# Two chunks of a layer's experts run as one stream of slot tiles, with a wait for GpSimd's second transfer of a step

## The reference, cut to what is computed

```python
x = x + linear_cumsum(layernorm(x))             # 8 sequences of 512 tokens, 128 wide
x = x + experts(layernorm(x))                    # 8 experts, 2 for each token
x = x + local_attention(layernorm(x))            # 16 heads, window of 128
x = x + experts(layernorm(x))                    # the same weights once more

# experts(x): xn = normalised x
probs = softmax(xn @ router_w.T / 1.5); w, idx = top_k(probs, 2)
h = silu(xn @ W1[e]);  y = h @ W2[e]             # 128 -> 512 -> 128
out = sum of w * y over the two experts, + x
```

## Time and profile before

| | |
|---|---|
| time of the kernel before | 985.13 us, median of 3 runs (983.61 to 986.66) |
| the profiled execution | 979.9 us, of which the span between first and last instruction is 977.8 us |
| PE busy | 684.0 us (70%) |
| DVE busy | 611.0 us (62%) |
| POOL busy | 435.3 us (45%) |
| ACT busy | 408.3 us (42%) |

### The profile page before, as it was taken

One profiled execution on the slowest core, in us unless ns is written; L12 is line 12 of the kernel. 1 busy time (PEld: TensorE's weight loads), 2 busy tenths in 40 slices (PEclk: granted clock), 3 DMA queues, 4 the chain that ended last, 5 costly groups with the idle time before them and its releaser, 6 DMA issues.

```text
span 977.8 us, 30500 instructions
## 1 busy us (share of the span) xinstructions
PE 684.0 (70%) x11616; PEld 523.8 (54%) x11616; DVE 611.0 (62%) x1840; ACT 408.3 (42%) x691; POOL 435.3 (45%) x409
## 2 busy tenths in 40 slices
PE   3811767797657677988888988877576777566770
PEld 2511556575545554655655656655375556455560
DVE  7888797854454557656656565677678544354444
ACT  1370245353333342754654655655354334233340
POOL 6591573484655600112122100050576766666661
PEclk9999977999988899999998999967767988798886
DMA  7210012132222221221211201001021111233114
GB/s 221 68 33 0 25 23 81 48 64 56 65 56 76 72 73 36 62 61 30 72 46 45 70 26 36 6 19 28 17 69 39 44 45 39 66 83 102 56 39 137
DMA packets 62923, 54.61 MB, mean 56 GB/s; under 512 B 10129, under 2 KB 55954, under 8 KB 62778
## 3 DMA queue, kind: packets, MB, share of 16 engines
q1 hardware_dynamic: 53250, 33.12, 11.8%
q0 software_dynamic: 9536, 19.55, 8.0%
HBM read 31.79 MB, written 20.84 MB: 54 GB/s over the span
## 4 chain that ended last, share of the span: by engine, by line
PE 43%; DVE 29%; issue 12%; another core or an unknown queue 6%; DVEq 4%; ACT 3%; DMA 2%; POOL 1%; SPq 0%; ACTq 0%; POOLq 0%
PE stbank L1109 6%; PE bank L1212 4%; PE stbank L1096 4%; PE sbank L1170 3%; DVE gl L767 3%; PE stbank L1110 3%; PE stbank L1098 3%; DVE zr L586 3%; DVE mx L825 2%; PE sbank L1165 2%; PE stbank L1196 2%; PE stbank L1097 2%; DVE ysb L757 2%; DVE xs L783 2%
## 5 line engine op out<-in xcount | busy, mean ns | idle before, releaser
L478 POOL DMA_INDIRECT xg<-table,idx x156 | 159.1, 1020 | 162.8 <-PE sbank L1077 66.4
L903 ACT ACTIVATE g<-stbank 128x512 f32<-128x512 f32 x156 | 93.3, 598 | 316.1 <-PE stbank L1098 242.5
L1109 PE MATMUL stbank<-wff,gh 128*128 x624 | 142.3, 306 | 112.0 <-DVE ysb L757 74.5
L757 DVE TENSOR_REDUCE ysb<-stbank 128x128 f32<-128x256 f32 x156 | 65.9, 423 | 152.4 <-remote 88.5
L1096 PE MATMUL stbank<-xT,wff 128*128 128x128 f16 x624 | 148.8, 246 | 17.3 <-issue 9.7
L825 DVE TENSOR_REDUCE mx<-sbank 128x2 f32<-128x320 f32 (+1 forms) x256 | 116.1, 472 | 68.6 <-PE sbank L1170 61.4
L950 ACT ACTIVATE pT<-stbank 128x1024 f32<-128x1024 f32 (+1 forms) x128 | 116.8, 917 | 81.4 <-PE stbank L1196 80.2
L1098 PE MATMUL stbank<-xT,wff 128*128 128x128 f16 x624 | 149.1, 246 | 0.0
L1097 PE MATMUL stbank<-xT,wff 128*128 128x128 f16 x624 | 146.5, 242 | 0.0
L1109 PEld LDWEIGHTS stbank<-wff,gh 128*128 128x128 f16 x624 | 67.5, 108 | 144.3 <-issue 126.6
L1110 PE MATMUL stbank<-wff,gl 128*128 x624 | 130.2, 239 | 0.0
(11 more groups left out here) (188 smaller groups left out, 1334.0 us busy)
## 6 DMA issues: line engine op xcount, KB each, us to landing
yslot<-ysb SPq DMA_DIRECT2D x78, 64.0 KB
table<-tb SPq DMA_DIRECT2D x16, 256.0 KB
cg<-ytab SPq DMA_DIRECT2D x16, 256.0 KB
qz<-dumps SPq DMA_DIRECT2D x96, 32.0 KB
kst<-dumps SPq DMA_DIRECT2D x96, 32.0 KB
xg<-table,idx POOLq DMA_INDIRECT x156
xs<-in_x SPq DMA_DIRECT2D x8, 256.0 KB, 4.6
qz<-in_w SPq DMA_DIRECT2D x1, 2048.0 KB, 10.4
```

Source lines behind the costliest of these rows:

```text
L478: g.indirect_dma_start(xg[:, i % G].rearrange("p a d -> p (a d)"), None, table[cc % 2], bass.IndirectOffsetOnAxis(ap=idx[:, cc % 2, t:t + ...
L903: a.activation(g32[:, i % 3, :], hbank[i % 2], ACT.Silu, scale=1.0 / WSCALE)
L1109: mm(o, gh[:, i % 3, P * f:P * f + P], whl, start=(f == 0), stop=False, skip_group_check=True)
```

## The change

The steps of a layer are one run of 88 (`range(2 * XSTEPS)`), and `layer_tile(layer, n)` gives the n-th of the layer's 78 tiles. Tiles of the second chunk follow those of the first without draining and filling. They end in step 82 where they ended in step 87. What runs beside stays at its steps: `beside(layer, s - XSTEPS)` from step 44 on. Beside step number k stood tile k of the second chunk at the transposes; now stands tile k + 5. Apart from this POOL gets a wait, `tile_under_way`: ahead of the scatter of a step (layer 1) and of the gather back of a step (layer 0) it waits for `s_h` of tile s-3, that is the end of the up projection that PE issues in step s-1.

```diff
@@ -205,6 +205,11 @@
         def tile_of(cc, t):
             return SLOT_TILES * cc + t
 
+        def layer_tile(layer, n):
+
+            i = tile_of(CHUNKS * layer, n)
+            return (i, i // SLOT_TILES, i % SLOT_TILES) if 0 <= n < CHUNKS * SLOT_TILES else (None, None, None)
+
         def scattered(slot, end):
 
             return (end - 1 - slot) // G - (tile_of(CHUNKS, 0) - 1 - slot) // G
@@ -239,16 +244,15 @@
 
 
             c0 = CHUNKS * layer
-            for s in range(XSTEPS):
-                x_step(c0, s)
-                if layer == 0:
+            for s in range(2 * XSTEPS):
+                x_step(layer, s)
+                if s >= XSTEPS:
+                    beside(layer, s - XSTEPS)
+                elif layer == 0:
                     a_step(1, s)
                     r_step(c0 + 1, s - A_BEFORE_R)
                 else:
                     r_step(c0 + 1, s)
-            for s in range(XSTEPS):
-                x_step(c0 + 1, s)
-                beside(layer, s)
 
         def front_in_attention(front, b, j):
...
+            def tile_under_way(layer, s):
+
+                i, _, _ = layer_tile(layer, s - 3)
+                if i is not None:
+                    pool.wait_ge(s_h, i + 1)
+
+            def x_step(layer, s):
+                if layer == 0 and ZERO_AT <= s < ZERO_AT + ZEROS:
 
                     if s == ZERO_AT:
                         pool.wait_ge(s_wl, 2)
@@ -467,23 +476,24 @@
                     n = 3 * NH * SEQ // ZEROS
                     z = qz[:].rearrange("p u h n -> p (u h n)")[:, n * (s - ZERO_AT):n * (s - ZERO_AT + 1)]
                     g.memset(z.bitcast(F32), 0.0).then_inc(s_zero, 1)
-                if s == 0:
-                    pool.wait_ge(s_idx, cc + 1)
-                    for i in range(2):
-                        pool.wait_ge(s_tbd[i], 16 * 2 * (cc + 1))
-                for t in range(AHEAD + 1) if s == 0 else (s + AHEAD,):
-                    if t < SLOT_TILES:
-                        i = tile_of(cc, t)
-                        wait(pool, s_xp, i - G + 1)
-                        g.indirect_dma_start(xg[:, i % G].rearrange("p a d -> p (a d)"), None, table[cc % 2],
-                                             bass.IndirectOffsetOnAxis(ap=idx[:, cc % 2, t:t + 1], axis=0)).then_inc(s_g[i % G], 16)
-
-                for t in (s - 6,) if s < XSTEPS - 1 else (s - 6, s - 5):
-                    if cc >= CHUNKS and t >= 0:
-                        i = tile_of(cc, t)
-                        pool.wait_ge(s_yc, i + 1)
-                        g.indirect_dma_start(ytab[cc % 2], bass.IndirectOffsetOnAxis(ap=sidx[:, cc % 2, t:t + 1], axis=0),
-                                             ysb[:, i % G, :], None).then_inc(s_sc[i % G], 16)
+                for n in range(AHEAD + 1) if s == 0 else (s + AHEAD,):
+                    i, cc, t = layer_tile(layer, n)
+                    if i is None:
+                        continue
+                    if t == 0:
+                        pool.wait_ge(s_idx, cc + 1)
+                        for k in range(2):
+                            pool.wait_ge(s_tbd[k], 16 * 2 * (cc + 1))
+                    wait(pool, s_xp, i - G + 1)
+                    g.indirect_dma_start(xg[:, i % G].rearrange("p a d -> p (a d)"), None, table[cc % 2],
+                                         bass.IndirectOffsetOnAxis(ap=idx[:, cc % 2, t:t + 1], axis=0)).then_inc(s_g[i % G], 16)
+
+                i, cc, t = layer_tile(layer, s - 6)
+                if layer and i is not None:
+                    tile_under_way(layer, s)
+                    pool.wait_ge(s_yc, i + 1)
+                    g.indirect_dma_start(ytab[cc % 2], bass.IndirectOffsetOnAxis(ap=sidx[:, cc % 2, t:t + 1], axis=0),
+                                         ysb[:, i % G, :], None).then_inc(s_sc[i % G], 16)
 
             def gather_back(b, m):
 
@@ -507,6 +517,7 @@
             def beside(layer, s):
                 m = gathered_back_at(s)
                 if layer == 0 and m is not None:
+                    tile_under_way(layer, XSTEPS + s)
                     gather_back(m // GATHERS, m % GATHERS)
                 if layer == 0 and prepared_at(s):
                     front(*prepared_at(s))
...
@@ -746,22 +757,22 @@
                     dve.drain()
                     v.tensor_tensor(sidx[:, cp, :], row, far, ALU.add).then_inc(s_idx, 1)
 
-            def x_step(cc, s):
-                if 0 <= s - 5 < SLOT_TILES:
-                    i = tile_of(cc, s - 5)
+            def x_step(layer, s):
+                i, _, _ = layer_tile(layer, s - 5)
+                if i is not None:
                     dve.wait_ge(s_y, i + 1)
                     if i - G < tile_of(CHUNKS, 0):
                         wait(dve, s_ys[i % G], 16 * (i // G))
                     else:
                         dve.wait_ge(s_sc[i % G], 16 * scattered(i % G, i))
                     v.tensor_reduce(ysb[:, i % G, :], ybank.rearrange("p (a d) -> p d a", a=2), AX.X, ALU.add).then_inc(s_yc, 1)
-                if s < SLOT_TILES:
-                    i = tile_of(cc, s)
+                i, _, _ = layer_tile(layer, s)
+                if i is not None:
                     dve.wait_ge(s_xp, i + 1)
                     wait(dve, s_h, i - 2)
                     v.tensor_copy(xT[:, i % 3, :], xbank[i % 2]).then_inc(s_xt, 1)
-                if 0 <= s - 3 < SLOT_TILES:
-                    i = tile_of(cc, s - 3)
+                i, _, _ = layer_tile(layer, s - 3)
+                if i is not None:
                     dve.wait_ge(s_gh, i + 1)
                     wait(dve, s_y, i - 2)
                     v.tensor_tensor(gl[:, i % 3, :], g32[:, i % 3, :], gh[:, i % 3, :], ALU.subtract).then_inc(s_gl, 1)
...
@@ -1065,31 +1076,31 @@
                     if k == 16:
                         ins.then_inc(s_ixp, 1)
 
-            def x_step(cc, s):
-                if s == 0:
-                    pe.wait_ge(s_wl, 2)
-                    pe.wait_ge(s_idx, cc + 1)
-                if s < SLOT_TILES:
-                    i = tile_of(cc, s)
+            def x_step(layer, s):
+                i, cc, t = layer_tile(layer, s)
+                if i is not None:
+                    if t == 0:
+                        pe.wait_ge(s_wl, 2)
+                        pe.wait_ge(s_idx, cc + 1)
                     pe.wait_ge(s_g[i % G], 16 * (i // G + 1))
                     wait(pe, s_xt, i - 1)
                     for a2 in range(2):
                         ins = pe.transpose(xbank[i % 2][:, P * a2:P * a2 + P], xg[:, i % G, a2, :], ident16[:])
                     ins.then_inc(s_xp, 1)
-                if s % LOADS == 0 and s < SLOT_TILES:
-
-                    n = min(LOADS, SLOT_TILES - s)
-                    _, ids = nc.values_load_multi_w_load_instructions(
-                        eid[0:1, cc % 2, s:s + n], [mybir.EngineType.PE], min_val=0, max_val=E - 1,
-                        skip_runtime_bounds_check_because="a count of thresholds passed, cut off at E - 1")
-                    for k in range(n):
-                        experts[s + k] = wff[:, bass.ds(ids[k], 1), :, :]
-                if 0 <= s - 2 < SLOT_TILES:
-                    i = tile_of(cc, s - 2)
+                    if t % LOADS == 0:
+
+                        n = min(LOADS, SLOT_TILES - t)
+                        _, ids = nc.values_load_multi_w_load_instructions(
+                            eid[0:1, cc % 2, t:t + n], [mybir.EngineType.PE], min_val=0, max_val=E - 1,
+                            skip_runtime_bounds_check_because="a count of thresholds passed, cut off at E - 1")
+                        for k in range(n):
+                            experts[i + k] = wff[:, bass.ds(ids[k], 1), :, :]
+                i, _, _ = layer_tile(layer, s - 2)
+                if i is not None:
                     pe.wait_ge(s_xt, i + 1)
                     wait(pe, s_gh, i - 1)
...
```

23 lines of the change are left out of this document (10 added, 13 removed).

## The result

| | before | after |
|---|---|---|
| median | 985.89 us (4 runs, 983.61 to 986.94) | 972.01 us (4 runs, 965.77 to 974.98) |
| profiled execution, its span | 979.9, 977.8 us | 965.77, 963.7 us |

The ratio is 0.9863, with a 95% interval of 0.9828 to 0.9899: a gain of 13.9 us in the medians and 14.1 us between the two profiled executions, where 20.6 were forecast.

A forecast was written before the change was run, and what follows sets the result against it. Bound by waits: runs of POOL's transfers, 1.43 us each, keep others from seeing what PE finished. Layer 1's seam -5.2, layer 0 -9.4, new wait -6: -20.6 from 985.1 gives 964.5 us, range 954 to 975.

The forecast's parts named there:

- (c): Layer 0, steps 31 to 38: without gathers they take 23.9 us instead of 30.53; -6.6 us, bounds -14.5 and 0.
- (e): End of layer 0: the V projection loses its cover, so the mask comes later; +1.9 us, other end 5.
- part 3: New wait before gathers back and scatters: a tile takes 2.94 us instead of 3.015; -6 us, bounds 0 and -13.
- Part 1: Layer 1, seam between chunks goes: 39 tiles take 117.6 us as a stream instead of 122.82; -5.2 us.
- Part 2: Layer 0: the seam goes and the work beside meets other tiles; -9.4 us in sum.
- (a): Layer 0, step 5 of the second half: its reduce comes at 244.8 instead of 240.63; +4.2 us.
- (b): Layer 0, steps 5 to 30 of the second half: same work, 85.75 us, unchanged without the new wait.
- (d): End of layer 0: the last reduce stands in step 38 instead of 43; -8.9 us.
- The wait does nothing: Both layers: the new wait brings nothing, only the seams' removal counts; 970.5 us; chance 0.20.
- The wait breaks the hold: Two-transfer steps: finished PE work gets through between POOL's transfers, 2.55 us a tile; 932.5 us, halfway 949; chance 0.14.
- The wait delays the scatters: Layer 1: the reduce waits for the delayed scatter's landing, 3.74 us a tile; 1011.8 us; chance 0.11.
- The gain of layer 0 doesn't come: Layer 0: steps 31 to 38 save nothing and its end costs 5 us; +0.3 there, 974 us; chance 0.10.

The follow-up runs named there:

- The stream alone: The changed kernel without the new wait in either layer, only the run of 78 tiles; 977.91 us, ratio 0.9921 to the kernel before.
- the long fill: The changed kernel, but in layer 1 POOL fills 520 unused columns behind each scatter instead of waiting ahead of it; 966.53 us, ratio 0.9886.
- two fills: The changed kernel, but in layer 1 POOL fills 256 unused columns behind each gather and each scatter, without the wait; 968.48 us, ratio 0.9909.
- POOL's plain store: The changed kernel, but in layer 1 POOL stores each tile's rows without indices in the scatter's place; 915.18 us.

## Why the prediction was right, and where its sizes were wrong

The forecast was -20.6 us, the measurement -13.9. The sign, the mechanism of layer 0 and the range held. The range was wide: the bounds of (c), (e) and part 3 even add up to 950 to 980 us, not to the 954 to 975 given, so that it held is weak evidence for the steps. Step by step:

**Part 1, the seam of layer 1 (-5.2): mis-sized, about -1.** The term was 39 tiles at 3.015 us against 122.82. The 3.015 came from 26 tiles of one execution. The stream alone ran at 3.11 in tiles 15 to 29, where its program is still that of the kernel before, and the other kernels with two indexed transfers and no fill there at 3.04 to 3.15. The kernel before itself has 2.99 in these tiles: 3.015 was the low side of what executions scatter. With 3.11 the term is 121.3 - 122.8 = -1.5 us. With the seam put back, the ratio rises by 0.1%, which the intervals don't tell from nothing. The step that failed is the pace: 3.11 us for a tile where 3.015 was said, 0.1 us on each of 39 tiles.

**Part 2, layer 0 (-9.4): right, and larger.** Its own steps, with the wait's share in them:
- (a) said +4.2, with 11 tiles at 2.0 us. They took 24.95 us (223.01 to 247.96), 2.27 each: tiles 35, 39 and 43 took 3.0 us, seven of the other eight 1.9 to 2.0, the last 2.4. The three are the tiles whose down projections stand in the steps in which PE loads four expert numbers (`t % LOADS == 0`); that these loads cost the 1 us is likely, but no run varied them. So tile 44's reduce stands 7.3 us behind the 240.63 of the earlier trace rows.
- (b) said 85.75 us unchanged (and -1.9 of part 3). It took 81.8 (247.96 to 329.80), -3.9; without the wait 83.6 and 84.8.
- (c) said 23.9 us for steps 31 to 38. They took 21.8 (329.80 to 351.60), -8.7 in the place of -6.6; without the wait 25.4 and 24.1, about as said.
- (d), 8.9 us, falls away as said: 7.3 - 3.9 - 8.7 - 8.9 = -14.2.
- (e) said that the mask follows the last reduce by 2.3 us in the place of 0.49. It follows by 2.67 (351.60 to 354.27), +2.2 where +1.9 was said (the terms given add up to 2.0). The first scores follow by 4.66 us where it was 1.57 (365.77 to 367.34), +3.1. Here the granted clock of PE counts, which the forecast left out: PE was busy for 1.91 of the 4 us up to 352, then the clock fell to the lower of its two levels (0.50, 1.2 GHz), and the four mask products took 1.87 us in the place of 1.04. In the seven kernels of the stream whose mask takes 1.02 us the scores follow by 3.81 to 3.87 us, so +2.3 without the clock. The stacks, the other end of (e), cost nothing: the scores start 0.12 us behind the mask's end. The stretch up to layer 1 is 1.5 us longer here; it lasts 352.2 to 359.3 us in the twelve kernels with the stream in layer 0, 355.9 in the mean, and 352.9 and 349.4 in the two without. So some of what layer 0 wins may be lost again there, which two executions can't settle.

```profile
354.27 1.87 PE L1263 MATMUL stbank<-mband,ident 128*128 128x512 f16 x4
...
356.26 0.43 PE L1181 MATMUL sbank<-kst,qz 127*32 127x128 f16 x8
```

The same scores in the kernel before, and the stretch after in which the clock fell (us, busy us of PE, PEld, DVE, ACT and POOL, granted clock, DMA):

```profile
367.34 0.29 PE L1170 MATMUL sbank<-kst,qz 127*32 127x128 f16 x8
```

```profile
352.00:356.00 4.00, 3.13 (x11) 1.51 (x10) 1.16 (x5) 1.05 (x5) 0.00 (x0) 0.50 0.55 175
```

**Part 3, the new wait (-6): right in sum, its mechanism not confirmed.** It is worth 0.9921 - 0.9863 = 0.6%, 5 to 6 us, with intervals that overlap a little. But it was to come from 0.075 us on each of 82 tiles. In layer 1 (57 of them, -4.3) a round with the wait isn't shorter (6.1 to 6.25 us for two tiles, 3.1 each, where 2.94 was said), and the profiled executions show nothing; only the medians show 4 us there, and only without the wait of layer 0. In layer 0 the profiled executions show some 4 us where 1.9 was said, in the steps of (b) and, to my surprise, of (c), where POOL issues gathers back alone. In the kernel before it brought nothing in layer 0 (365.5 against 365.8). Why it works only beside the stream no run settles. That the sum came out near 6 is luck as far as its working goes.

**The rivals.** "The wait does nothing" is refuted for the whole; for layer 1 it is open. "The wait breaks the hold" fell: idle times of 3.5 us remain. "The wait delays the scatters" fell for this change, and came true with the long fill. "The gain of layer 0 doesn't come" fell.

**The rule that spoke against part 3.** With SP's plain store in the scatter's place, the same bytes land and a tile costs 2.04 in the place of 3.1 us. POOL's indexed transfers do hold what PE has finished. The Trainium skill ("SBUF — State Buffer", section "Who interferes with whom") says that PE and ACT never wait on anyone and that a DMA never contends with a compute engine. It speaks of ports of SBUF; the traces show only that others go on late after PE is done, not which part of the chip holds them. By its rule, as the prediction took it, the plain store would have gained nothing; the measurement decides against it.

## What to carry to other kernels

Count the transfers with index lists that POOL issues close behind each other, not their rows or bytes. In this kernel one alone held nothing back, while a run of them held what the matrix engine had finished for some 1.4 us each, up to the end of the run, and one fewer in a step was worth 1 us for each step. Merging two pipelines saves the seam only where the seam is slower than the stream: here the draining ran free of the hold, so in layer 1 nothing was won, and in layer 0 the win came from the seam's own steps and from tiles that now stand beside other work. And a pace read from 26 tiles of one execution is not good to 0.1 us; multiplied by 57 or 82 tiles, that is the whole forecast.

## What the hardware showed beside this

**The hold by the transfer.** 64 rows took 0.91 us to issue and 128 rows 0.99, and both held equally; a plain store issued by POOL took 0.58 us and held nothing; neither did an indexed transfer that stood alone.

**A transfer that starts while DVE subtracts is longer.** In the kernel with the fill of 520 columns the subtraction (`gl`, two inputs in SBUF) began at 802.11 and the scatter at 802.20:

```profile
802.11 0.68 DVE L783 TENSOR_TENSOR gl<-g,gh 128x512 f16<-128x512 f32 x1
802.20 1.45 POOL L499 DMA_INDIRECT ytab<-ysb,sidx  x1 [0.30 <-DVE ysb L773]
```

It took 1.45 in the place of 0.99 us: 0.46 more, where 0.59 us of the subtraction were left. With two fills:

```profile
804.08 0.68 DVE L785 TENSOR_TENSOR gl<-g,gh 128x512 f16<-128x512 f32 x1
804.35 1.28 POOL L501 DMA_INDIRECT ytab<-ysb,sidx  x1 [0.17 <-issue]
```

0.28 more, with 0.41 left. Each time the excess ends about 0.13 us before the subtraction does, as if the transfer could read its indices only then; no run shows that it is the indices. In all the traces together, 406 indexed transfers began inside a subtraction with 0.3 us or more of it left and took 1.09 to 1.50 us; 122 began in its first 0.034 us and took 0.94 to 1.00; and 646 began up to 0.5 us ahead of one and took 0.91 to 1.04. One of the last is a gather that began 0.18 us ahead (799.95, in the kernel with POOL's plain store) and took its usual 0.97. The Trainium skill ("GPSIMD Engine Reference", section "1. Specifications") says that POOL's way to SBUF is shared with DVE and that DVE instructions with two SBUF inputs contend for it; the traces agree for a transfer that starts during one.
